# The row of relative destinations of a graph layer: one transfer from memory for four quads in place of a product for each

## What is computed

```
h = max(layernorm(x), 0)
e = concat(h[src], h[dst])                     # 200000 x 128
m = relu(e @ W1 + b1) @ W2 + b2                # 200000 x 64
s, cnt = segment_sum(m, dst), segment_sum(1, dst)
x = x + s / max(cnt, 1)
```

## Time and profile before

| | |
|---|---|
| median of three timed runs | 2404.67 us (2403.09 to 2406.99) |
| the profiled execution's own time | 2396.18 us |
| its span (first to last instruction) | 2394.3 us |
| PE busy | 1461.8 us, 61% |
| PEld busy | 1222.6 us, 51% |
| DVE busy | 923.1 us, 39% |
| ACT busy | 352.1 us, 15% |
| POOL busy | 1476.8 us, 62% |
| DMA | 136.93 MB, mean 57 GB/s |

### The profile page before, as it was taken

The page is one execution under the profiler, slowest core; times in us unless marked ns, Lnnn a source line. Parts: engine busy times, 40 slices in busy tenths (PEclk is TensorE's granted clock), DMA queues, the critical chain, the costliest instruction groups (busy, mean ns, idle before and its releaser), DMA issues.

```text
span 2394.3 us, 23165 instructions
## 1 busy us (share of the span) xinstructions
PE 1461.8 (61%) x8389; PEld 1222.6 (51%) x8390; DVE 923.1 (39%) x2278; ACT 352.1 (15%) x704; POOL 1476.8 (62%) x1572
## 2 busy tenths in 40 slices
PE   4541656666665665566565555566566666567699
PEld 3331545555555554455454445455455555455577
DVE  7241433323333233343333333343333333334366
ACT  3230111111111111111111111111111111111122
POOL 5646666666666666666666666666666666666610
PEclk9775777777677777877777887677777777887899
DMA  6531111111111111211221121121122221222210
GB/s 150 152 92 52 48 49 50 49 50 48 48 50 48 50 48 49 53 50 52 60 52 51 52 53 51 47 64 52 50 53 60 52 52 51 56 65 56 58 40 22
DMA packets 107754, 136.93 MB, mean 57 GB/s; under 512 B 30864, under 2 KB 81847, under 8 KB 107635
## 3 DMA queue, kind: packets, MB, share of 16 engines
q0 software_dynamic: 50016, 101.22, 16.3%
q1 hardware_dynamic: 57055, 33.95, 5.3%
q10 hardware_dynamic: 564, 0.23, 0.0%
HBM read 119.21 MB, written 16.07 MB: 56 GB/s over the span
## 4 chain that ended last, share of the span: by engine, by line
another core or an unknown queue 43%; PE 25%; issue 15%; DVE 15%; ACT 2%; DVEq 1%
PE bank L988 8%; PE bank L977 7%; DVE g L755 5%; DVE work L742 4%; PE bank L967 3%; PE bank L1003 2%; PE bank L995 2%; DVE work L735 2%; PE bank L867 1%; DVE raw_t L735 1%; DVE acc L761 1%; PE bank L1013 1%; ACT g L542 1%; DVE stats L609 0%
## 5 line engine op out<-in xcount | busy, mean ns | idle before, releaser
L421 POOL DMA_INDIRECT g<-p_table,src_e x1523 | 1437.2, 944 | 776.6 <-issue 421.9
L988 PE MATMUL bank<-work,g 128*128 128x128 f32 x3126 | 586.3, 333 | 135.5 <-issue 134.5
L988 PEld LDWEIGHTS bank<-work,g 128*128 128x128 f32 x3126 | 503.7, 238 | 205.7 <-issue 203.0
L542 ACT ACTIVATE g<-g 128x512 f32<-128x512 f32 x391 | 246.2, 630 | 1334.3 <-DVE g L755 1069.0
L735 DVE TENSOR_SCALAR_CACHE_REDUCE work<-bank,rows_f 128x512 f32<-128x512 f32 (+1 forms) x261 | 195.0, 747 | 458.4 <-remote 277.3
L977 PEld LDWEIGHTS bank<-work 128*128 128x128 f32 x2086 | 344.1, 234 | 21.1 <-issue 5.6
L977 PE MATMUL bank<-work 128*128 128x128 f32 x2086 | 341.3, 317 | 8.6 <-issue 8.6
L967 PE MATMUL bank<-rel_q,ident 128*128 128x512 bf16 x391 | 185.2, 474 | 259.3 <-DVE work L735 123.6
L1003 PE MATMUL bank<-sums_u,w 128*64 128x128 f32 x398 | 105.4, 355 | 314.5 <-ACT sums_u L547 224.9
L761 DVE TENSOR_TENSOR acc<-acc,bank 65x128 f32 x199 | 55.8, 281 | 581.5 <-remote 521.1
L755 DVE TENSOR_TENSOR g<-bank,g 128x512 f32<-128x512 f32 x391 | 267.7, 685 | 0.0
(11 more groups left out here) (93 smaller groups left out, 420.8 us busy)
## 6 DMA issues: line engine op xcount, KB each, us to landing
g<-p_table,src_e POOLq DMA_INDIRECT x1523
work<-q_table SPq DMA_DIRECT2D x199, 64.0 KB
p_table<-g SPq DMA_DIRECT2D x12, 448.0 KB
q_table<-work SPq DMA_DIRECT2D x12, 448.0 KB
out_dram<-xs SPq DMA_DIRECT2D x5, 448.0 KB
xs<-in_x_dram SPq DMA_DIRECT2D x2, 672.0 KB
xs<-in_x_dram SPq DMA_DIRECT2D x1, 784.0 KB
acc<-in_src_dram SPq DMA_DIRECT2D x1, 768.0 KB
```

The lines of the kernel that those rows point to most:

```text
L421: nc.gpsimd.indirect_dma_start(out=g[:, slot(n), j * HID:(j + 1) * HID], out_offset=None, in_=p_table, in_offset=bass.IndirectOffsetOnAxis ...
L542: nc.scalar.activation(g[:, slot(n), 0:w], g[:, slot(n), 0:w], ACT.Relu).then_inc(r_done, 1)
L988: last = nc.tensor.matmul(u_bank[i % 2][:, 0:WIN], g[:, slot(n), HID * c:HID * (c + 1)], member[:, n % MEMBERS, c, :], start=n == GROUPS[i ...
```

## The change

The row of a quad no longer comes from a product. When rel_q is computed, SP writes it once to a table in DRAM (rel_table, 512 rows of 512 bf16). In the main loop SP issues, for every four quads, one DMA that reads four rows of the table (4 KB) and writes them to all 128 partitions, 512 KB in all, into one of two buffers: rel_q itself and rows_b, a new tile whose first part also takes over the place of hs. It waits until the spreads of the quads that used the buffer are done. The spread reads its row from SBUF in bf16 instead of PSUM in f32. The semaphore row_done, broadcast_rows, ident16 and its copy go. PSUM bank 4 becomes a fourth z bank, and w1's place a fourth spread buffer; counts are kept for 16 quads. DVE does the spread of n + 3 and PE spread_q of n + 2, each one quad further ahead.

```diff
+    rel_table = nc.dram_tensor("rel_table", [QT * 128, QE], BF16).ap()
-        ident16 = sb("ident16", [128, 128], BF16)
+        rows_b = sb("rows_b", [128, 4 * QE], BF16)
+        hs = rows_b[0:NP, :].bitcast(F32).rearrange("p (k t f) -> p k t f", k=HS, f=FEAT)
+        rows_of = [rel_q[:, :, :].rearrange("p t e -> p (t e)"), rows_b[:, :]]
-        z_bank, u_bank, row_bank = [bank[0], bank[1], bank[5]], bank[2:4], bank[4]
+        z_bank, u_bank, turn_bank = [bank[0], bank[1], bank[4], bank[5]], bank[2:4], bank[4]
...
+            sp.wait_ge(row_table, QT)
+            sp.dma_start(rel_table.rearrange("(t q) e -> q t e", q=128), rel_q[:, :, :]).then_inc(rel_out, 16)
...
+            def load_rows(j):
+                if j >= 2:
+                    sp.wait_ge(spread_done, 4 * (j - 1))
+                sp.dma_start(rows_of[j % 2], rel_table[4 * j:4 * j + 4, :].rearrange("(o q) e -> o (q e)", o=1)
+                             .to_broadcast([128, 4 * QE])).then_inc(rows_there[j % 2], 16)
+
             def fast():
                 stores = 0
+                sp.wait_ge(rel_out, 16)
                 for n in range(QUADS):
+                    if n % 4 == 0:
+                        load_rows(n // 4)
...
             def spread_of(n):
-                dve.wait_ge(row_done, n + 1)
-                nc.vector.tensor_scalar(spreads[n % 3][:, 0:w], row_bank[:, 0:w], rows_f[:, :], 0.0,
+                if n % 4 == 0:
+                    dve.wait_ge(rows_there[n // 4 % 2], 16 * (n // 8 + 1))
+                row = QE * (n % 4)
+                nc.vector.tensor_scalar(spreads[n % 4][:, 0:w], rows_of[n // 4 % 2][:, row:row + w], rows_f[:, :], 0.0,
...
             def fast():
-                spread_of(0)
-                spread_of(1)
+                for n in range(3):
+                    spread_of(n)
...
-                    if n + 2 < QUADS:
-                        spread_of(n + 2)
+                    if n + 3 < QUADS:
+                        spread_of(n + 3)
...
-            def broadcast_rows(n):
-                w = 128 * chunks_of(n)
-                if n:
-                    pe.wait_ge(spread_done, n)
-                nc.tensor.matmul(row_bank[:, 0:w], ident16[:, n % 128:n % 128 + 1].to_broadcast([128, 128]),
-                                 rel_q[:, n // 128, 0:w], start=True, stop=True).then_inc(row_done, 1)
...
             def fast():
-                broadcast_rows(0)
-                broadcast_rows(1)
                 spread_q(0)
+                spread_q(1)
                 for n in range(QUADS + 3):
                     if n + 2 < QUADS:
-                        broadcast_rows(n + 2)
-                    if n + 1 < QUADS:
-                        spread_q(n + 1)
+                        spread_q(n + 2)
```

More of the change, by code:

```diff
@@ L41 @@
 MEMBERS = 4
-COUNTS = 8
+COUNTS = 16
 GROUP_SIZES = ((128, 4), (320, 2), (QT * 128, 1))
@@ L175, in gnn_kernel @@
         member = work[:, 1024:3072].rearrange("p (k c w) -> p k c w", k=MEMBERS, c=4)
-        spreads = [work[:, 3072:3584], work[:, 3584:4096], raw_t[:, :, :, :].rearrange("p n k e -> p (n k e)")]
+        spreads = [work[:, 3072:3584], work[:, 3584:4096], raw_t[:, :, :, :].rearrange("p n k e -> p (n k e)"),
+                   w1[:, :, :, :].rearrange("p a b h -> p (a b h)")]
         windows_of = member[0:1, 1, :, :].rearrange("o c w -> o (c w)").bitcast(I32)
         bank = [ctx.enter_context(nc.psum_tensor(f"bank{i}", [128, 512], F32)) for i in range(8)]
-        z_bank, u_bank, row_bank = [bank[0], bank[1], bank[5]], bank[2:4], bank[4]
+        z_bank, u_bank, turn_bank = [bank[0], bank[1], bank[4], bank[5]], bank[2:4], bank[4]
         o = bank[7][0:NP, WIN:WIN + BT * (FEAT + 1)].rearrange("p (t f) -> p t f", t=BT)
@@ L185, in gnn_kernel @@
         h_bank, rows_bank = bank[0:2], (bank[2:4], bank[4:6])
-        idents, consts, pads, w1_zero, eps_there, zeroed, ident16_done, fold_done = sems(
-            "idents consts pads w1_zero eps_there zeroed ident16_done fold_done")
+        idents, consts, pads, w1_zero, eps_there, zeroed, fold_done = sems(
+            "idents consts pads w1_zero eps_there zeroed fold_done")
         w_in, b1_in, w2_in, b2_in, idx_in, src_in, dst_in, q_pad = sems(
@@ L210, in gnn_kernel @@
         gathered = [sem(f"gathered{k}") for k in range(RING)]
+        rel_out = sem("rel_out")
+        rows_there = [sem(f"rows_there{k}") for k in range(2)]
         window_in = [sem(f"window_in{k}") for k in range(WINDOWS)]
-        row_done, spread_done, zq_done, z_done, r_done, u_psum, u_copied, v_psum, v_done = sems(
-            "row_done spread_done zq_done z_done r_done u_psum u_copied v_psum v_done")
+        spread_done, zq_done, z_done, r_done, u_psum, u_copied, v_psum, v_done = sems(
+            "spread_done zq_done z_done r_done u_psum u_copied v_psum v_done")
         o_psum, most_done, inverse_done, mean_done, out_done = sems("o_psum most_done inverse_done mean_done out_done")
@@ L560, in window_general @@
                     act.wait_ge(m_turned, m)
-                    nc.scalar.copy(spreads[0], row_bank[:, :]).then_inc(m_spread, 1)
+                    nc.scalar.copy(spreads[0], turn_bank[:, :]).then_inc(m_spread, 1)
                     act.wait_ge(z_made, m)
@@ L579, in _ @@
             nc.vector.tensor_copy(fold[:, :], ident[0:FEAT + 1, 0:FEAT + 1]).then_inc(fold_done, 1)
-            nc.vector.tensor_copy(ident16[:, :], ident[:, :]).then_inc(ident16_done, 1)
             nc.vector.memset(sums[:, ZERO_DVE[0]:ZERO_DVE[1]], 0.0).then_inc(v_zero, 1)
@@ L695, in _ @@
                 quads, lows = base[:, first:to].rearrange("p (k j) -> p k j", j=size), real[:, first:first + shape[1]]
-                nc.vector.tensor_reduce(lows, bank[0][:, first:to].rearrange("p (k j) -> p k j", j=size), AX.X, ALU.min)                    .then_inc(lows_done, 1)
+                nc.vector.tensor_reduce(lows, bank[0][:, first:to].rearrange("p (k j) -> p k j", j=size), AX.X, ALU.min)\
+                    .then_inc(lows_done, 1)
                 dve.wait_ge(lows_done, k + 1)
@@ L754, in add_rows @@
                     dve.wait_ge(gathered[slot(n)], rows_landed(n))
-                nc.vector.tensor_tensor(rows_n, z_bank[n % 3][:, 0:w], rows_n, ALU.add).then_inc(z_done, 1)
+                nc.vector.tensor_tensor(rows_n, z_bank[n % 4][:, 0:w], rows_n, ALU.add).then_inc(z_done, 1)
             def add_sums(i, at):
@@ L955, in _ @@
             pe.wait_ge(b2_in, 16)
-            pe.wait_ge(row_table, QT)
-            pe.wait_ge(ident16_done, 1)
             pe.wait_ge(dst_table, QT)
@@ L976, in spread_q @@
                 for c in range(chunks_of(n)):
-                    last = nc.tensor.matmul(z_bank[n % 3][:, HID * c:HID * (c + 1)],
-                                            spreads[n % 3][:, 128 * c:128 * (c + 1)], qw[:, i % WINDOWS, :],
+                    last = nc.tensor.matmul(z_bank[n % 4][:, HID * c:HID * (c + 1)],
+                                            spreads[n % 4][:, 128 * c:128 * (c + 1)], qw[:, i % WINDOWS, :],
                                             start=True, stop=True)
@@ L1040, in window_general @@
                     for c in range(4):
-                        last = nc.tensor.transpose(row_bank[:, 128 * c:128 * (c + 1)], member[:, 0, c, :], ident[:, :])
+                        last = nc.tensor.transpose(turn_bank[:, 128 * c:128 * (c + 1)], member[:, 0, c, :], ident[:, :])
                     last.then_inc(m_turned, 1)
```

1 line of the change is left out of this document (removed).

## The result

The changed kernel takes 2392.09 us (median of 7 runs, 2384.49 to 2394.52), the kernel before 2403.09 us on the same chip (7 runs, 2397.22 to 2407.10). The ratio is 0.995, with a 95% interval of 0.9932 to 0.9967: 11 us less, where the interval allows 8 to 16. The prediction said 6 less, the same way but less than the interval allows. The profiled execution of the changed kernel took 2393.35 us.

A forecast was written before the change was run, and what follows sets the result against it. Prediction: POOL's gathers, paced by late tensor engine counts, bound the middle; the tensor engine bounds the end stage. Terms -7.0 and +1 gave -6.0 on the 2404.7 us median: 2398.7 us, range 2384 to 2418.

The forecast's parts named there:

- The row product: Removing the tensor engine's product for each quad: -7.0 us in the end stage, 0 in the middle.
- first term: End stage: 32 row products of 0.22 us gone from the tensor engine, -7.0 us.
- second half: Middle of the loop: the product's 0.38 us is covered by 8 us of tensor engine idle time, 0.
- The spread from SBUF: Vector engine reading the row from SBUF: 0, with +41 us as upper end if it held up POOL's gathers.
- Rival C: Spread from SBUF holds POOL up, or transfers cost by their bytes: about 2415 to 2439 us; 12%.
- The transfers: 98 row transfers of 512 KB, 89 beside gathers: +1 us, with 0 and +17 as ends.
- Rival B: Row transfers slower than the quads they feed, so it ends slower: +75 us at 20 us each, +290 at 25; 9%.
- rival D: Transfers eat the gain, middle +3 to +12 us: 2401 to 2410 us; 23%.
- The waits on SP: Row transfers waiting in SP's queue for their buffer's last spreads: hidden, unless a transfer takes too long.
- The start: Table write and read under the first train of gathers, three spreads early: 0, at best -11 us.
- Four buffers: Four spread and z buffers, tensor engine one quad further ahead: 0 in the middle and in the end stage.
- law of pace: Main loop: late tensor engine counts make POOL stop, so gathers average 1.441 us however many quads a round completes.

The follow-up runs named there:

- e7: e2 with the row product run only for quads 0 to 354, not in the end stage: 2418.29 us, ratio 0.9970 to the kernel before.
- e2: e1 with the row product run again for every quad, into a bank nobody reads: 2421.54 us, ratio 0.9997 to the kernel before.
- e9: e2 with four row products per quad in place of one: 2433.49 us, ratio 1.0123 to the kernel before.
- e1: Changed kernel with three z banks and three spreads, engines running ahead as before the change: 2406.67 us, ratio 0.9943 to the kernel before.
- e3: Changed kernel with only the first two of the 98 row transfers: 2405.48 us, ratio 0.9934 to the kernel before.
- e8: Changed kernel with gathers bringing 256 of the 512 bytes of each row from quad 36 on: 2416.44 us.
- e11: Changed kernel with gathers bringing 64 of the 128 rows from quad 36 on: 2411.52 us.
- e4: Changed kernel with POOL's lead falling one quad per two, from 36 to 10: 2373.79 us, ratio 0.9793 to the kernel before.
- e10: e5 with POOL waiting only at every fourth quad, every second from quad 272: 2428.55 us, ratio 1.0117 to the kernel before.
- e5: e4 with POOL's lead falling one quad per four from quad 270, to 6: 2355.81 us, ratio 0.9712 to the kernel before.
- e12: Kernel before, row product kept, with e5's falling lead: 1982.55 us, ratio 0.9999 to the kernel before on the same chip.

## Why the prediction was right, and where it was not

1. **The row product.** Its first term, -7.0 in the end stage, was measured at -6.7, -7.9, -8.9 (e7 against e2) and -7.1 (e9). Its second half failed: "in the middle the product's 0.38 is covered by the 8 us in which the tensor engine is idle anyway: 0". Outside the end stage a product costs 3.1 (1.4 to 4.1) by the medians of e9, and that is also what the pair leaves: 11 less the 6.7 of the end stage is 4, within 1 to 10. This is the mis-sized term. The profiled middles give 1.8, 3.5, 2.6 to 5.1 and 5.2, but they differ by as much between kernels without a product (2041.2 in the changed kernel, 2056.2 to 2060.3 in e1, e3, e8 and e11), so they don't show where in the loop the time lies. How it comes about is argued and not shown: an engine that is idle in the mean of a round may still be busy in that part of the round that others wait for. The rows of e4 and e10 show such a part: what the sums have not finished by a stop costs POOL a longer stop. End stage and the rest together are some 10, for 11 between the medians of the pair; the 15 between e2 and e1 lie above that, with intervals that allow 7 to 19.
2. **The spread from SBUF.** Gathers have a mean of 946 ns (944 before) with one spread of 735 ns for every four gathers: 0, as predicted. The rule cited there from the Trainium skill (SBUF — State Buffer, "Who interferes with whom") stands as far as this trace can show: the form with the accumulator didn't hold POOL up. Rival C fell.
3. **The transfers.** Predicted +1. No run gives this term by itself: e3 against the changed kernel, across two chips, allows -2 to 10, and e3 against e1 (1.2 of medians) changes the buffers too. The bound is e2: with transfers, spread source and product it is at 0.9997 of the kernel before (0.9984 to 1.0009), so -4 to +2 us in all. Rival B fell, as no spread waited for a row; rival D fell by the time, 2392 where it had 2401 to 2410.
4. **The waits on SP** were hidden: idle time ahead of L754 is 0.0.
5. **The start** gave nothing. The long stop is 11.30 where it was 11.50, although three spreads could go before it.
6. **Four buffers** gave nothing: 0.9943 with three, 0.995 with four. They did make rounds longer. Of the rounds that begin between 250 and 1990 us in the timeline of POOL, 49 have 16 and 29 have 12 gathers, where the kernel before has 30 and 53 and e1 29 and 51, and by the law it made no difference to the pace.

So the gain was undersized by 5 us, of which some 3 are the product's share outside the end stage; the direction and the range held. The law of pace held in every group of runs but the last, with rounds of 16 at 23.0 in the pair and 23.2 in e1 to e8, except where POOL was made to ask for more quads than a stop brings (e4, e5, e10). But the prediction used it as if it were part of the kernel, and e12 shows that it is not; had the pair been timed on that chip, the reasons given would not apply. That the pair was timed where the law holds, as four of the five groups were, was in part luck. What the change is worth there was not measured: its kernel did not run there.

What stays open is what makes the tensor engine's counts late in those groups and not in the last, and why each gather costs 1.44 there, whatever it moves.

The best version is e5: 0.9712 of the kernel before on a chip with late counts. On the chip without them the same line, on the kernel before, neither helps nor hurts (0.9999).

## What to carry to other kernels

Where a ring of buffers is full at the end of a gather-bound loop, its contents are an end stage that another engine works off alone. Compute taken off that engine pays there by the instruction (0.22 us x 32), and a lead that shrinks before the end pays more (85 us off the end stage for 30 in the middle). Slack that is idle on average need not be a cover: read which part of a round the others wait for before you price removed work at nothing. A profiled execution is one sample: the middles of kernels without the product ran from 2041 to 2060 us over several chips, so a difference of a few us is better read from medians of one chip. Before building on an odd delay in the trace, run the unchanged kernel on a second chip; a law that fits a trace to 0.5% may not belong to the kernel.

## What the hardware showed that I had not expected

- The kernel before took 2403 to 2427 us (medians) in four groups of runs and 1983 us in the fifth, which ran on another chip, with the same 946 ns a gather and 1.25 instead of 1.44 us from one to the next.
- In the groups of runs with late counts the round of POOL has a length set by the number of gathers, 23.0 to 23.2 us for 16, whether each moves 128 rows of 512 bytes, 128 rows of 256 bytes (pace 1.453 in e8, 1.451 in e1) or 64 rows of 512 bytes. When the instructions get shorter, the stop gets longer.
- Rounds of 8 gathers take 11.8 us and those of 16 take 23.0, so short stops are nearly free (0.3 us for each two quads), but asking for more quads than a stop brings costs 3 us (e4) or 7 (e10).
- Reading the same 4 KB of memory into all 128 partitions, 98 times 512 KB, left no mark beyond a few us on a kernel that is busy with gathers (e2, which has them, is within 4 us of the kernel before).
